# Delta-rule stage: single transfers per tile in a tiled DRAM layout, and another order of all five engines

## The reference

```python
k, q, v = (_short_conv(x @ W.T + b, w_conv, b_conv) for each of the three)   # conv over 4 tokens
beta = sigmoid(x @ Wbeta.T + bbeta)                                          # one per head
k, q, v = k / (knorm + EPS), q / (qnorm + EPS), silu(v) / (knorm + EPS)
def step(S, inp):                                                            # S: 32 x 32, 16 heads
    q_t, k_t, v_t, b_t = inp
    pred = einsum('bhk,bhkv->bhv', k_t, S)
    S = S + b_t * (k_t[..., None] * (v_t - pred)[..., None, :])
    o_t = einsum('bhk,bhkv->bhv', q_t, S)
    return (S, o_t)
_, o = scan(step, 0, (q, k, v, beta))
x = _layernorm(x + _rmsnorm(o, norm_w) @ Wo.T + bo)
```

## Time and profile before

| | us |
|---|---|
| median of 3 runs | 3028.76 |
| the profiled execution | 3036.44 |
| its span (first to last instruction) | 3034.6 |
| PE, DVE, ACT, POOL busy | 2599.5, 2234.0, 1414.8, 472.0 |
| delta stage | 0 to about 1093 |
| context stage | about 1097 to 1830 |

### The profile page before, as it was taken

One profiled execution on the slowest core, in us unless ns is written; L12 is line 12 of the kernel. 1 busy time (PEld: TensorE's weight loads), 2 busy tenths in 40 slices (PEclk: granted clock), 3 DMA queues, 4 the chain that ended last, 5 costly groups with the idle time before them and its releaser, 6 DMA issues. The chain is left out here.

```text
span 3034.6 us, 86658 instructions
## 1 busy us (share of the span) xinstructions
PE 2599.5 (86%) x35310; PEld 1836.3 (61%) x35332; DVE 2234.0 (74%) x3969; ACT 1414.8 (47%) x2560; POOL 472.0 (16%) x661
## 2 busy tenths in 40 slices
PE   7788888888887669999999983997589999987998
PEld 5666666666665447677667652443366676764665
DVE  3898887888889516777787765987678878760787
ACT  6666656666665102222223224544356565541454
POOL 2232223222223000000000000005500000000122
PEclk9899999999998679999999996998899999998999
DMA  3001111111110140111111115528931221214332
GB/s 90 10 18 31 32 58 31 31 31 32 59 32 25 45 168 22 49 40 45 55 55 55 48 35 192 180 104 289 278 106 56 71 68 55 76 35 160 111 126 77
DMA packets 229344, 233.98 MB, mean 77 GB/s; under 512 B 24082, under 2 KB 157842, under 8 KB 229012
## 3 DMA queue, kind: packets, MB, share of 16 engines
q1 hardware_dynamic: 229012, 229.18, 23.6%
HBM read 136.32 MB, written 92.81 MB: 76 GB/s over the span
## 5 line engine op out<-in xcount | busy, mean ns | idle before, releaser
L710 ACT ACTIVATE delta_product<-delta_line,delta_conv_w 128x256 f32<-128x256 f32 x576 | 247.1, 497 | 0.0
L1246 PE MATMUL ctxatt_banks<-ctxatt_xT,ctxatt_wq 128*128 128x256 f32 x1024 | 232.4, 380 | 2.9 <-ACT ctxatt_qT L1322 2.1
L1285 PE MATMUL ctxatt_banks<-ctxatt_wo,ctxatt_oT 128*128 128x512 f32 x512 | 229.4, 601 | 4.9 <-DVE ctxatt_norm_y L1391 4.9
L1246 PEld LDWEIGHTS ctxatt_banks<-ctxatt_xT,ctxatt_wq 128*128 128x128 f32 x1024 | 189.5, 190 | 28.5 <-ACT ctxatt_qT L1322 3.3
L944 DVE TENSOR_TENSOR delta_t_sys<-delta_t_sys,delta_squares 128x30 f32<-128x30 f32 (+14 forms) x480 | 173.8, 362 | 16.7
L941 DVE TENSOR_TENSOR delta_squares<-delta_t_sys 128x30 f32<-128x30 f32 (+14 forms) x480 | 173.9, 362 | 12.0
L447 POOL TENSOR_TENSOR delta_product<-delta_product 128x1024 f32<-128x1024 f32 x48 | 117.3, 2444 | 320.1 <-ACT delta_product L710 320.1
L1285 PEld LDWEIGHTS ctxatt_banks<-ctxatt_wo,ctxatt_oT 128*128 128x128 f32 x512 | 95.7, 192 | 116.1 <-issue 109.5
L1332 ACT ACTIVATE ctxatt_probsT<-ctxatt_banks 128x512 f32<-128x512 f32 x128 | 69.4, 594 | 203.2 <-PE ctxatt_banks L1267 203.2
L2166 PE MATMUL wkv_banks<-wkv_woT,wkv_oT 128*128 128x512 f32 x256 | 133.3, 681 | 36.0 <-DVE wkv_oT L2364 36.0
L702 ACT ACTIVATE delta_conv<-delta_line,delta_conv_b,delta_conv_w 128x256 f32<-128x256 f32 x192 | 111.8, 591 | 99.8 <-DVE delta_v_tok L892 99.8
(11 more groups left out here) (341 smaller groups left out, 6239.7 us busy)
## 6 DMA issues: line engine op xcount, KB each, us to landing
h<-ffn_hid SPq DMA_DIRECT2D x66, 256.0 KB, 2.0
ffn_hid<-h SPq DMA_DIRECT2D x6, 1536.0 KB, 10.0
wkv_xT<-xT SPq DMA_DIRECT2D x64, 129.0 KB, 2.8
delta_xT<-xT SPq DMA_DIRECT2D x64, 128.0 KB
delta_x<-x SPq DMA_DIRECT2D x16, 512.0 KB
xT<-delta_newT SPq DMA_DIRECT2D x64, 128.0 KB
x<-delta_new SPq DMA_DIRECT2D x16, 512.0 KB
ctxatt_xT<-xT SPq DMA_DIRECT2D x64, 128.0 KB, 2.6
```

Of the source, the lines that this page charges most:

```text
L710: made = act.activation(slot(n, i)[:, j - 1, g].rearrange("p (b t) -> p b t", b=B), line[:, i, g, :, j:j + P], ACT.Copy, scale=conv_w[:, i ...
L1246: mm = pe.matmul(b_q[:, i * B * P:(i + 1) * B * P], wq[:, k, pair * P:(pair + 1) * P], xT_sb[:, n.parity, k], start=k == 0, stop=k == KB - 1)
L1285: mm = pe.matmul(b_o[:], oT[:, b, k, :], wo[:, k, :], start=k == 0, stop=k == PAIRS - 1)
```

## The change

It does four things. `xT` of the input and `xT[0]`, the delta stage's output, get the layout `(S // P, P, KB, B * P)`, so that one tile is one transfer with 4 KB per partition, for the delta stage's loads and stores and for the context stage's loads. The host lays the input out so (a transposition, no arithmetic). SP loads `x` for t3 instead of t2. The lists of PE, ACT, DVE and POOL get another order; the steps listed are the same ones, and steps at a list's end may appear at the next one's start with a higher tile offset. The waits are the same but for the counts of the transfers.

```diff
-        xT_view = xT_in.rearrange("(k p) b t -> p k b t", p=P)
-        xT_out_view = xT_out.rearrange("(k p) b t -> p k b t", p=P)
+        xT_view = xT_in.rearrange("s p k n -> s p (k n)")
+        xT_out_view = xT_out.rearrange("s p k n -> s p (k n)")
...
+                def load_columns(n):
+                    wait(sp, projected, n, len(GROUPS), -len(GROUPS))
+                    sp.sem_inc(passed, 1)
+                    sp.dma_start(xT_sb[:, n.parity].rearrange("p k n -> p (k n)"), xT_view[n.slot()].rearrange("s p n -> (s p) n")).then_inc(xT_here[n.parity], 16)
...
+                def load_rows(n):
+                    wait(sp, norm.done, n, norm.OPS, norm.SUMMED - norm.OPS)
...
+                def store(n):
+                    wait(sp, newT_kept, n, B, B)
+                    sp.sem_inc(passed, 1)
+                    sp.dma_start(xT_out_view[n.slot()].rearrange("s p n -> (s p) n"), newT[:].rearrange("p k b t -> p (k b t)")).then_inc(newT_stored, 16)
+                    sp.dma_start(x_out_view[tokens(n)], new[:]).then_inc(new_stored, 16)
...
                 def step(n):
-                    if n:
-                        wait(sp, projected, n, len(GROUPS), -len(GROUPS))
-                        sp.sem_inc(passed, 1)
-                        for k in range(KB):
-                            sp.dma_start(xT_sb[:, n.parity, k].rearrange("p (b t) -> p b t", b=B), xT_view[:, k, :, tokens(n)]).then_inc(xT_here[n.parity], 16)
...
-                    if t := n.back(2):
-                        wait(sp, norm.done, t, norm.OPS, norm.SUMMED - norm.OPS)
-                        sp.sem_inc(passed, 1)
-                        sp.dma_start(x_sb[:], x_view[tokens(t)]).then_inc(x_here, 16)
-                    if t := n.back(4):
-                        wait(sp, newT_kept, t, B, B)
-                        sp.sem_inc(passed, 1)
-                        for k in range(KB):
-                            sp.dma_start(xT_out_view[:, k, :, tokens(t)], newT[:, k]).then_inc(newT_stored, 16)
-                        sp.dma_start(x_out_view[tokens(t)], new[:]).then_inc(new_stored, 16)
+                    t1, t2, t3, t4 = n.back(1), n.back(2), n.back(3), n.back(4)
+                    if n:
+                        load_columns(n)
+                    if t3:
+                        load_rows(t3)
+                    if t4:
+                        store(t4)
...
-                        here(pe, xT_here, n, 16 * KB)
+                        here(pe, xT_here, n, 16)
...
-                        for k in range(KB):
-                            sp.dma_start(xT_sb[:, n.parity, k].rearrange("p (b t) -> p b t", b=B), xT_view[:, k, :, tokens(n)]).then_inc(xT_here[n.parity], 16)
+                        sp.dma_start(xT_sb[:, n.parity].rearrange("p k n -> p (k n)"), xT_view[n.slot()].rearrange("s p n -> (s p) n")).then_inc(xT_here[n.parity], 16)
...
-    xT = [scratch(f"xT_{k}", (D, B, S + (k == 2))) for k in range(5)]
+    xT = [scratch(f"xT_{k}", (D, B, S + (k == 2)) if k else (S // P, P, KB, B * P)) for k in range(5)]
```

More of the change, by code:

```diff
@@ L601, in step @@
                     t1, t2, t3, t4 = n.back(1), n.back(2), n.back(3), n.back(4)
+                    if t3:
+                        update(t3, 2)
+                    if t1:
+                        project(t1, 11)
+                    if t3:
+                        step_state(t3, 2)
+                    if t4:
+                        project_out(t4, 0)
+                    if t3:
+                        outputs(t3, 1)
+                        predict(t3, 3)
+                    if t4:
+                        project_out(t4, 1)
+                    if t3:
+                        outputs(t3, 2)
                     if t1:
@@ L604, in step @@
                     if t3:
+                        update(t3, 3)
                         step_state(t3, 3)
@@ L619, in step @@
                     if t2:
-                        update(t2, 0)
+                        step_state(t2, 0)
                     if n:
@@ L766, in step @@
                     t1, t2, t3, t4 = n.back(1), n.back(2), n.back(3), n.back(4)
+                    if t1:
+                        taps(t1, 9)
+                        taps(t1, 10)
+                        keep_kq(t1, 0)
                     if t3:
@@ L797, in step @@
                     if t1:
-                        square(t1, 1)
+                        take_root(t1)
                     if n:
-                        first_tap(n, 1)
-                        first_tap(n, 2)
+                        keep(n, 2)
+                        taps(n, 1)
                     if t3:
@@ L816, in step @@
                     if n:
+                        first_tap(n, 3)
+                        keep(n, 4)
                         taps(n, 3)
                         first_tap(n, 4)
+                        keep(n, 5)
+                        first_tap(n, 5)
+                    if t4:
+                        keep_new(t4, 0)
+                    if n:
+                        taps(n, 4)
+                    if t1:
+                        gate(t1)
+                    if n:
                         keep(n, 6)
-                        keep(n, 7)
-                        taps(n, 4)
-                        first_tap(n, 5)
+                        taps(n, 5)
                     if t2:
@@ L825, in step @@
                     if n:
+                        keep(n, 7)
+                        first_tap(n, 6)
+                        taps(n, 6)
                         keep(n, 8)
-                        first_tap(n, 6)
-                        taps(n, 5)
-                    if t4:
-                        keep_new(t4, 0)
-                    if n:
                         first_tap(n, 7)
-                    if t2:
-                        keep_u(t2, 2)
-                    if n:
+                        keep(n, 9)
                         first_tap(n, 8)
@@ L1006, in step @@
                     t1, t2, t3 = n.back(1), n.back(2), n.back(3)
+                    if t3:
+                        rms_sum(t3)
                     if t1:
-                        sum_squares(t1, 1)
+                        invert_norms(t1)
                     if t3:
@@ L1048, in step @@
                     if t1:
-                        solve(t1, 5)
+                        turn(t1, 2)
+                    if n:
+                        join(n, 0, 1)
+                        join(n, 1, 0)
                     if t3:
@@ L1072, in step @@
                     if n:
-                        join(n, 1, 1)
+                        turn(n, 0)
                     if t1:
                         solve(t1, 14)
+                    if t3:
+                        add(t3, 1)
+                    if t1:
                         from_systems(t1)
@@ L1083, in step @@
                     if n:
-                        turn(n, 1)
                         sum_squares(n, 0)
-                    if t2:
-                        rms_sum(t2)
+                        sum_squares(n, 1)
                     if isinstance(n.index, int) and n.index == 0:
```

163 lines of the change are left out of this document (65 added, 98 removed).

## The result

| | before | after |
|---|---|---|
| median of 4 runs, us | 3030.81 (3025.34 to 3035.20) | 2986.55 (2985.33 to 2991.48) |
| the profiled execution, us | 3036.44 | 2985.33 |
| its span, us | 3034.6 | 2983.3 |
| mean granted clock | 0.928 | 0.939 |

The ratio is 0.986, with a 95% interval of 0.984 to 0.988: 44 us less by the medians, where 59 were forecast (2970 us, with 8 chances in 10 for 2940 to 3003). In the kernel after, PE's lines of the delta stage are numbered 8 higher (L514 is L522, L544 is L552) and DVE's 3 higher (L941 is L944, L965 is L968).

What follows compares the result with a forecast made beforehand. A loop DVE, SP, PE, DVE was taken to set the 63.4 us beat, with DVE's 58.8 next: 12 x (63.4 - 58.8) = 55, plus 4 at the edges, 59 us less. Forecast 2970 us, 8 in 10 for 2940 to 3003.

Steps and rivals of the forecast that it cites:

- The bound: Delta stage: a loop DVE, SP, PE, DVE sets the beat, 10.4 + 9.3 + 43.7 = 63.4 us a tile.
- SP's order and the cover: SP's queue: with `load_rows` at t3, `xT` lands with over 10 us of cover; PE's wait costs nothing.
- The clock: PE in the delta stage: 3.2 us of busy time a tile go with the wait, 54.2 to 51.0.
- The beat: DVE in the delta stage: 51.7 floor + 1.0 jump + 4.5 port + 1.6 waits = 58.8 us a tile.
- The port: DVE instructions stretched by POOL through the shared port: 4.5 us a tile, from 3.4 to 6.0.
- The loop's jump: Jump back of DVE's loop in the delta stage: stays, 1.0 us a tile over 12 tiles.
- The last stretch: Drain of the delta stage after the last projection: change of 0, bounds -6 and +6 us.
- The edges: First `xT` load and last `newT` store, one issue each: 2 us saved at either end, 4 in all.
- The sum: Whole kernel: 12 tiles x (63.4 - 58.8) = 55, plus 4 at the ends: 59 us less.
- rival 3: DVE beside POOL: the shared port decides, 62.3 us a tile, 3012 us in all; chance 0.15.
- Rival 5: Head of ACT's queue holds up the next tile's first matmul, 64.4 us a tile, 3041 us; chance 0.06.
- Rival 4: SP's queue: `keep_new` comes late, `xT` lands after PE is ready, within 4 us of 3025; chance 0.05.

Runs made afterwards that it cites:

- e2: Kernel before with one edit, SP loads `x` for t3 instead of t2: 3006.85 us, 0.990 of before.
- e4: Kernel after, but SP loads `x` for t2 again: 3169.49 us, 1.044 of before.
- e8: Kernel after with beta's projection done twice on PE, 8 matmuls more a tile: 2992.21 us, 0.986 of before.
- e10: Kernel after, unchanged, run and profiled again on another chip: 2993.68 us, 0.986 of before.
- e7: Kernel after with one more DVE instruction a tile, a sum of 128x1024 that nobody reads: 2991.84 us, 0.986 of before.
- e5: Kernel after with the four engines' old lists from step 16 on, behind the last tile's projections: 2987.42 us, 0.985 of before.
- e11: e9 with the lists of the kernel before behind the last tile: 2974.58 us, 0.980 of before.
- e9: e6 with DVE's list written out for all tiles instead of looped: 2976.71 us, 0.981 of before.
- e12: e9 with `turn(t1, 2)`, a transpose, moved ahead of `solve(t1, 6)`: 2972.28 us, 0.979 of before.
- e6: Kernel after without DVE's maximum with 1e-30 in `sum_squares`, 1e-30 added under ACT's root instead: 2971.17 us, 0.981 of before.

## Why the prediction was right, and where it was off

*The bound.* Right. The loop from `add` over SP to PE set the old beat. Opening it at one place (e2) ends the wait, and closing it again in the kernel after (e4) brings it back, larger.

*SP's order and the cover.* Right: the load was to be issued over 10 us ahead, and it is 18.3; with 5.8 us to land, over 12 us of cover are left. One step was wrong, without cost: `load_rows` does not "pass at once". By SP's sums of waits from 600 to 720 after, it waits about 24 us for the second `add`, which now stands late in DVE's turn. The store behind it would have waited longer in any case, for `keep_new`:

```profile
SPq L415 <- ACT delta_newT L730: 60.7, 2, 30.8
SPq L410 <- DVE delta_norm_y L1001: 48.6, 2, 24.8
```

*The clock.* Right in kind: the first group runs at the higher level, and the granted clock rose from 0.94 to 0.98. Of the 3.2 us of PE's busy time 2.1 came back (54.2 to 52.1), since the clock did not reach 1.00. That cost little, since 1.3 us more of PE's work moved the beat by 0.2 (e8).

*The beat.* 58.8 was forecast, 58.9 measured, with terms that were partly off and cancelled: that it fits to 0.1 is luck, and e10 has 59.6. The port term is measured at 5.8 where 4.5 was forecast, DVE's waits of 0.1 us and more at 1.7 (the jump's 0.4 among them) where 2.6 was, which leaves 58.9 - 5.8 - 1.7 = 51.4 as the floor, where 51.7 was.
- *The port.* The size lay inside the bounds of 3.4 to 6.0, the places did not. I moved 1.4 us from L908 to the products of `rms_invert`; they stayed at 0.19 us (0.35 for L988's). `pair_taps` against `solve` was 2.0, as forecast. The term for the third `pair_taps`, "near `rms_sum`: 0 to 1.6", is 1.8 and fell on L904, an instruction that I had not listed because it has one input. `join` costs 1.7 (1.3 beside `mask_beta`, 0.4 beside `add_bias`), where I had 0 to 1 for `add_bias` alone.
- The Trainium skill ("SBUF — State Buffer", "Who interferes with whom") says of `tensor_scalar` too that it can take the shared pair, in a mode that uses both ports, and can then contend with GpSimd. By this rule, the trace agrees: L904 is a `tensor_scalar` and took 2.01 us beside `pair_taps`, 0.19 without. I had drawn only on the rule for two inputs.
- *The loop's jump.* I had 1.0 us a tile; it is 4.3 / 11 = 0.4. In the kernel before, the row ahead of the jump ended at 722.57 and the next began at 725.54; after, L904 is still running while the sequencer jumps, and only 1.05 us are left bare. In e7, where L904 ends sooner, `issue` rises to 8.5 us in the same 4 times. So the two terms hide each other.

*The last stretch.* This term of the sum was mis-sized: 0, with bounds of -6 and +6, and it measured +7.9. The marks that I had laid explain half of it. I measured from PE's first matmul. Another mark is DVE's transpose of a tile's solved system, at the end of a turn in both orders; here those of tiles 2 and 13, from the timelines before and after:

```profile
207.77 1.98 DVE L955 STREAM_TRANSPOSE delta_tT<-delta_t_sys 128x1024 f32<-128x1024 f32 x1
...
901.61 1.93 DVE L955 STREAM_TRANSPOSE delta_tT<-delta_t_sys 128x1024 f32<-128x1024 f32 x1
```
```profile
207.35 1.92 DVE L958 STREAM_TRANSPOSE delta_tT<-delta_t_sys 128x1024 f32<-128x1024 f32 x1
...
854.99 1.91 DVE L958 STREAM_TRANSPOSE delta_tT<-delta_t_sys 128x1024 f32<-128x1024 f32 x1
```

By these the stretch to the stage's end is 188.5 us before (1090.1 - 901.61) and 192.4 after (1047.4 - 854.99): +3.9. The other 4.0 are PE running further ahead of DVE at tile 15 than at tile 4, a gain that the PE-based beat books and the end takes back. DVE's beats are 693.84 / 11 = 63.1 and 647.64 / 11 = 58.9: 46.2 us in eleven beats, where 63.4 - 58.8 had been taken twelve times for 55.

The 3.9 that are left are not settled. Over the last stretch PE is busy 3.9 us longer and the mean clock is 0.74 instead of 0.75; the stretch repeats (199.0 in e10). The old lists at the end shorten it in both pairs (e5 by 2.6, e11 against e9 by 7.2), but the medians move by about 2 us or less (e11 against e9 on one chip, within the intervals), and e8, with the new lists, has 190.1. From e5 to e12 it goes with the granted clock of the stretch, whatever the lists: 190.1 to 194.2 us at 0.77 or 0.78 (e7, e8, e11, e12), 195.9 to 199.4 at 0.73 to 0.75 (e5, e6, e9, e10). Whether the low clock makes the stretch long, or the idle time of a long stretch lowers the clock, is open.

*The edges.* 2 us were forecast at either end. The first matmul comes 0.6 us earlier (12.87 to 12.24), but at 13.07 in e10, so nothing is shown there. From the stage's end to the first transfer of the context stage it is 5.4 us instead of 6.9, and 5.4 again in e10. At most 2 of 4.

*The sum*, from the profiled executions: -0.4 up to the first DVE mark, -46.2 in eleven beats, +3.9 in the last stretch, -1.5 at the stage's end: -44.2. To 59 it lacks 14.8: 8.8 in the beats, the largest part (55 forecast for twelve; DVE's old beat is 63.1 and not 63.4, and the twelfth lies in the last stretch), 3.9 in the last stretch, 2.1 at the edges. The stages behind took 7.1 us less in this execution (1930.5 of 1937.6), 4.8 of them in the last stage, which the change does not touch; the medians, 44.3 apart, do not show them.

*The rivals.* The port as the decider (rival 3) went half-way: it took 1.3 us more than my term, it is larger than DVE's waits (5.8 against 1.7), and e6 and e12 gained by taking 1.3 and 2.1 us off it. Rival 5's head of ACT's queue did not come: PE waits 6.0 us in six times for `delta_line`. Rival 4 is excluded by the missing wait.

## What to carry to other kernels

When a queue closes a loop between engines, look for the one instruction that waits for the late event, and move it to a turn in which the event has already come; fewer issues in front of the transfer bought 1.1 us of a beat here, while the same bytes stood ahead of it. Price the new order from the most tightly packed turn of the old one, not from means over turns with waits in them, and take the beat on the engine that will set it, since another engine's mark drifts against it. List for the shared port every DVE instruction that lies beside a POOL instruction, those with one input too, and put a transpose or a sum over the free axis there.

## What the runs showed of the hardware that I had not expected

- A `tensor_scalar` of 128x64 with one SBUF input was held until POOL's two-input product ended: 2.01 us for 0.19. Work put ahead of it on DVE took the place of the wait: 1.21 us were added, and the held instruction fell by 1.07, to 0.90.
- Nor is POOL the one that always wins: its `scale_outputs` takes 1.91 us in the earlier trace rows and 2.89 at 693.72, where DVE's `join` of 2.55 us was under way.
- DVE's jump back is bare for 2.97 us behind a short instruction, and for 1.05 behind one that runs for 2.01 us.
- Four transfers of 512 KB issued in 2.9 us (577.53 to 580.47) had the last one landed 5.1 us after its issue ended, at 325 GB/s and a share of 0.85. Transfers in fours, in pieces of 512 bytes, went at a lower rate (202 GB/s at 0.63; over the same 2 MB from the issue of `x` to PE's start 207 against 259). Number and layout changed together, so which of them sets the rate is not shown.
